# Quantiser without split signs and two tiles in turns in the last feed-forward part; key products in quarters, ahead of their shift, in the local attention

## The reference

```python
_GRID = [0.0, 0.5, 1.0, 1.5, 2.0, 3.0, 4.0, 6.0]
def fp4_quant_dequant(x):          # blocks of 16 along the last dimension
    scale = max(abs(xb)) / 6.0, at least 1e-12
    xn = xb / scale
    q = _GRID[searchsorted(_MID, abs(xn))] * sign(xn) * scale
gate = fp4_linear(x, w_gate)       # 128 -> 352
y = fp4_linear(x, w_up)            # 128 -> 352
h = silu(gate) * y
return fp4_linear(h, w_down)       # 352 -> 128
```

```python
bk, bv = look_around(bk), look_around(bv)     # the window before and the own one
sim = einsum('bhwid,bhwjd->bhwij', bq, bk)
mask = (i < j) | (i > j + WINDOW) | (j == -1)
attn = softmax(where(mask, -max, sim))
out = einsum('bhwij,bhwjd->bhwid', attn, bv)
```

## Time and profile before

| | us |
|---|---|
| median of 3 runs | 4181.39 |
| lowest and highest | 4177.72, 4183.64 |
| the profiled execution's own time | 4167.43 |
| its span (first to last instruction) | 4165.7 |
| TensorE busy (72% of the span) | 3015.8 |
| VectorE busy (61%) | 2557.0 |
| ScalarE busy (35%) | 1448.0 |
| GpSimd busy (19%) | 787.8 |

### The profile page before, as it was taken

The page is one execution under the profiler, slowest core; times in us unless marked ns, Lnnn a source line. Parts: engine busy times, 40 slices in busy tenths (PEclk is TensorE's granted clock), DMA queues, the critical chain, the costliest instruction groups (busy, mean ns, idle before and its releaser), DMA issues. The chain is left out here.

```text
span 4165.7 us, 87048 instructions
## 1 busy us (share of the span) xinstructions
PE 3015.8 (72%) x34526; PEld 2091.1 (50%) x34526; DVE 2557.0 (61%) x7026; ACT 1448.0 (35%) x2873; POOL 787.8 (19%) x759
## 2 busy tenths in 40 slices
PE   4567887886547788788554778878856477787885
PEld 3434565654434456565443445656535244565653
DVE  6674565557676456555757745764575764566457
ACT  4134433422404344342240434434224044343421
POOL 3132211101213221110121322121012132111110
PEclk7579999997657899899765889999976588999996
DMA  1011000000001100000000110000000011000000
GB/s 37 6 38 30 14 3 2 14 20 1 7 6 38 30 14 3 2 14 20 1 7 6 40 30 12 3 2 18 16 1 7 6 40 30 11 3 2 19 14 6
DMA packets 65264, 59.65 MB, mean 14 GB/s; under 512 B 16403, under 2 KB 54212, under 8 KB 64838
## 3 DMA queue, kind: packets, MB, share of 16 engines
q1 hardware_dynamic: 63606, 53.24, 4.7%
q10 hardware_dynamic: 1232, 0.61, 0.1%
HBM read 36.29 MB, written 2.10 MB: 9 GB/s over the span
## 5 line engine op out<-in xcount | busy, mean ns | idle before, releaser
L157 POOL TENSOR_TENSOR ln_rstd<-ln_var_eps,neghalf 128x4 f32<-128x4 f32 x128 | 130.1, 1017 | 1223.6 <-DVE ln_var_eps L169 1188.5
L1188 POOL TENSOR_TENSOR l1t_ss<-l1t_ss,neghalf 128x16 f32<-128x16 f32 x64 | 243.7, 3808 | 478.8 <-DVE l1t_ss L1222 478.8
L2103 ACT ACTIVATE l2r_P<-l2r_bank_score 128x512 f32<-128x512 f32 x320 | 173.7, 594 | 176.3 <-PE l2r_bank_score L1825 176.3
L2103 ACT ACTIVATE l2a_P<-l2a_bank_score 128x512 f32<-128x512 f32 x320 | 173.7, 594 | 168.7 <-PE l2a_bank_score L1825 168.7
L1395 PE MATMUL l1t_ring<-l1f_qkv,x_normT 128*128 128x512 f32 x384 | 218.8, 699 | 13.1 <-ACT x_normT L1095 13.1
L1995 DVE CUSTOM_DVE_ANT_0 l2r_masked<-l2r_bank_ring,l2r_neg_wide 128x512 bf16<-128x512 f32 (+1 forms) x256 | 148.7, 622 | 76.7 <-PE l2r_bank_ring L1794 76.4
L1995 DVE CUSTOM_DVE_ANT_0 l2a_masked<-l2a_bank_ring,l2a_neg_wide 128x512 bf16<-128x512 f32 (+1 forms) x256 | 149.0, 622 | 73.9 <-PE l2a_bank_ring L1794 72.6
L1825 PE MATMUL l2a_bank_score<-l2a_q_head,l2a_k_head 32*128 32x128 f32 x2560 | 188.3, 284 | 2.4 <-DMA l2a_q_head<-l2a_shiftT 1.0
L1794 PE MATMUL l2r_bank_ring<-l2r_k_head,l2r_q_head 32*128 32x128 f32 x2432 | 174.6, 286 | 19.9 <-DVE l2r_m L1995 9.8
L1794 PE MATMUL l2a_bank_ring<-l2a_k_head,l2a_q_head 32*128 32x128 f32 x2432 | 176.7, 286 | 16.4 <-DVE l2a_m L1995 7.1
L1825 PE MATMUL l2r_bank_score<-l2r_q_head,l2r_k_head 32*128 32x128 f32 x2560 | 186.0, 282 | 2.6 <-DMA l2r_q_head<-l2r_shiftT 1.2
(11 more groups left out here) (616 smaller groups left out, 7949.6 us busy)
## 6 DMA issues: line engine op xcount, KB each, us to landing
l1t_v_low<-l1t_v SPq DMA_DIRECT2D x112, 130.0 KB, 2.3
l2e_w<-in_L_ffn_w SPq DMA_DIRECT2D x96, 128.0 KB, 2.3
l1f_qkv<-in_L_ffn_wqkv SPq DMA_DIRECT2D x8, 768.0 KB, 4.5
l1f_tables<-in_l_tables SPq DMA_DIRECT2D x8, 512.0 KB, 6.0
l1f_w<-in_L_ffn_w SPq DMA_DIRECT2D x8, 341.0 KB
x_in<-in_L_attn_hidden_states SPq DMA_DIRECT2D x10, 256.0 KB, 3.5
l1f_wo<-in_L_ffn_wo SPq DMA_DIRECT2D x8, 256.0 KB, 4.8
l2a_q_head<-l2a_shiftT SPq DMA_DIRECT2D x128, 2.0 KB
```

The source lines that it names most:

```text
L157: pool.tensor_tensor(b.rs[:, p, :], b.ve[:, p, :], b.neghalf[:, 0:NT], ALU.pow).then_inc(s["post_rstd"] if post else s["pre_rstd"], 1)
L1188: pool.tensor_tensor(ss[:, n % 2], ss[:, n % 2], b.neghalf[:, 0:2 * H8], ALU.pow).then_inc(s["rn_ready"], 1)
L2103: act.activation(self.P[:, use % self.P_RING].rearrange("k h q -> k (h q)"), self.score_bank(h, g)[:, :], ACT.Exp, scale=self.scale).then_ ...
```

## The change

In the last feed-forward part the quantiser is replaced by `fp4_in_turns`, which takes one or two tiles and gives every step to each tile in turn; a step waits for the last step of its own tile only (`Turns`). It rounds the signed value, without the magnitude and without putting the sign back. The tiles go in the groups (0), (1, 2), (3, 4), (5, 6), (7). The gate and up product of tile 0 stand ahead of the second sequence's transposes, and TensorE and ScalarE follow the groups. The up products now wait for h itself (`h_ready`) and not for the quantised h.

In the local attention the keys of a score tile change places: its rows 0 to 63 are the first 64 keys of the own tile, which all 128 queries use, its rows 64 to 127 the last 64 keys of the tile before for the first 64 queries, and the second 64 keys of the own tile for the others. So a chunk takes, for each row half of the array, one product of 64 keys with 128 queries and two with 64. Mask and key products come first and are placed before the output of the tile before; the shift is added last, in `subtract`. The masks `neg_k` and the layout of `v_low` follow.

```diff
+def fp4_in_turns(dve, turns, jobs, ready, dst_read=()):
...
+    for i, (src, dst, am, inv, v, pw, r) in jobs:
+        turns.wait(i)
+        turns(i, dve.tensor_scalar(pw.bitcast(U32), v.bitcast(U32), EXPONENT, None, ALU.bitwise_and))
+    for i, (src, dst, am, inv, v, pw, r) in jobs:
+        turns.wait(i)
+        turns(i, dve.tensor_scalar(pw, pw, 1.0, magic, ALU.max, ALU.mult))
+    for i, (src, dst, am, inv, v, pw, r) in jobs:
+        turns.wait(i)
+        turns(i, dve.scalar_tensor_tensor(r, v, 1.0 - 2.0 ** -24, pw, ALU.mult, ALU.add))
...
@@ l1_ffn_attention, sync
-                sync.dma_start(v_low[64:128, p, j], v[0:64, p, j]).then_inc(s["v_low_ready"], 16)
+                sync.dma_start(v_low[0:64, p, j], v[0:64, p, j]).then_inc(s["v_low_ready"], 16)
...
@@ l1_ffn_attention, tensor
             def scores(n):
                 j, p = tiles[n]
-                pe.wait_ge(s["q_ready"], n + 1)
-                pe.wait_ge(s["k_ready"], n + 1)
-                pe.wait_ge(s["shiftT_ready"], n + 1)
                 if n:
                     pe.wait_ge(s["p_ready"], 2 * n)
...
+                pe.wait_ge(s["q_ready"], n + 1)
+                pe.wait_ge(s["k_ready"], n + 1)
+                for c in range(CHUNKS):
+                    at = 128 * c
+                    for half, here, keys, queries in ((0, 0, j * 128 + 64, slice(0, 128)), (1, 0, j * 128, slice(0, 64)),
+                                                      (1, 64, j * 128 + 128, slice(64, 128))):
+                        for u in range(2):
+                            rows = slice(64 * u, 64 * u + 64)
+                            pe.matmul(s_bank[u][64 * half:64 * half + 64, at + here:at + queries.stop],
+                                      k[rows, p, c, keys:keys + 64], q[rows, n % 2, c, queries], start=False, stop=True,
+                                      skip_group_check=True)
+
+            def subtract(n):
+                p = tiles[n][1]
+                pe.wait_ge(s["shiftT_ready"], n + 1)
...
             for n in range(T):
-                scores(n)
+                subtract(n)
...
+                if n + 1 < T:
+                    scores(n + 1)
                 if n:
                     turn_output(n - 1)
...
@@ l3_ffn, scalar
+            gate(0)
+            for k, members in enumerate(groups):
+                for n in groups[k + 1] if k + 1 < len(groups) else ():
+                    gate(n)
+                for n in members:
+                    copy_h(n)
...
@@ l3_ffn, tensor
+            turn_x(0)
+            gate_up(0)
+            turn_x(1)
+            for k, members in enumerate(groups):
+                for n in groups[k + 1] if k + 1 < len(groups) else ():
+                    gate_up(n)
+                for n in members:
+                    turn_h(n)
+                for n in members:
+                    down(n)
```

More of the change, by code:

```diff
@@ L814, with __init__, wait, __call__ @@
 FP4 = Quantizer(16, 6.0, 1e-12, 1.0 / 2, signed=False)
+class Turns:
+    def __init__(self, eng, sem, n):
+        self.eng, self.steps, self.done = eng, Steps(eng, sem), [0] * n
+    def wait(self, i):
+        if self.done[i]:
+            self.eng.wait_ge(self.steps.sem, self.done[i])
+    def __call__(self, i, ins):
+        self.steps(ins)
+        self.done[i] = self.steps.n
+def fp4_in_turns(dve, turns, jobs, ready, dst_read=()):
+    block, unit = 16, 1.0 / 2
+    magic = 1.5 * 2.0 ** 23 * unit
+    def blocks(a):
+        return a.rearrange("p (n k) -> p n k", k=block)
+    def spread(a):
+        return a.unsqueeze(2).to_broadcast([a.shape[0], a.shape[1], block])
+    jobs = list(enumerate(jobs))
+    for i, (src, dst, am, inv, v, pw, r) in jobs:
+        turns.wait(i)
+        turns(i, dve.tensor_reduce(am, blocks(src), AX, ALU.max, apply_absolute_value=True))
+    for i, (src, dst, am, inv, v, pw, r) in jobs:
+        turns.wait(i)
+        turns(i, dve.tensor_scalar(am, am, 1.0 / 6.0, 1e-12, ALU.mult, ALU.max))
+    for i, (src, dst, am, inv, v, pw, r) in jobs:
+        turns.wait(i)
+        turns(i, dve.reciprocal(inv, am))
+    for i, (src, dst, am, inv, v, pw, r) in jobs:
+        turns.wait(i)
+        turns(i, dve.tensor_tensor(blocks(v), blocks(src), spread(inv), ALU.mult))
+    for i, (src, dst, am, inv, v, pw, r) in jobs:
+        turns.wait(i)
+        turns(i, dve.tensor_scalar(pw.bitcast(U32), v.bitcast(U32), EXPONENT, None, ALU.bitwise_and))
+    for i, (src, dst, am, inv, v, pw, r) in jobs:
+        turns.wait(i)
+        turns(i, dve.tensor_scalar(pw, pw, 1.0, magic, ALU.max, ALU.mult))
+    for i, (src, dst, am, inv, v, pw, r) in jobs:
+        turns.wait(i)
+        turns(i, dve.scalar_tensor_tensor(r, v, 1.0 - 2.0 ** -24, pw, ALU.mult, ALU.add))
+    for i, (src, dst, am, inv, v, pw, r) in jobs:
+        turns.wait(i)
+        turns(i, dve.tensor_tensor(r, r, pw, ALU.subtract))
+    for i, (src, dst, am, inv, v, pw, r) in jobs:
+        turns.wait(i)
+        if dst_read and dst_read[i][1]:
+            dve.wait_ge(*dst_read[i])
+        dve.tensor_tensor(blocks(dst), blocks(r), spread(am), ALU.mult).then_inc(ready, 1)
 def l0_ffn_weights(nc, ctx, b, a):
@@ L1031, in l1_ffn_constants @@
         own(pool.tensor_copy(m[64:128, :], w.neg_low[64:128, :]))
+    own.settle()
+    own(pool.memset(w.neg_low[:], 0.0))
+    keep(w.neg_low[:, 0:64], [[-1, 64]], -64, 1, fill=MASKED)
     for first, m in enumerate(w.neg_k):
-        keep(m[:], [[0, 2], [-1, 64]], 0, 1, fill=MASKED)
-        keep(m[:], [[0, 2], [1, 64]], 64, -1, fill=MASKED)
-        if first:
-            keep(m[:, 0:64], [[0, 64]], -64, 1, fill=MASKED)
+        keep(m[:, 64:128], [[-1, 64]], 0, 1, fill=MASKED)
+        keep(m[:, 64:128], [[1, 64]], 64, -1, fill=MASKED)
+        keep(m[:, 0:64], [[1, 64]], 0, -1, fill=MASKED)
+        if not first:
+            own.settle()
+            own(pool.tensor_copy(m[64:128, 0:64], w.neg_low[64:128, 0:64]))
     keep(w.sel[:], [[-1, H8], [0, 128]], 0, 1, ALU.not_equal, 1.0)
@@ L1184, in _ @@
             own(pool.memset(k_bf[:, :, :, 0:64], 0.0))
-            own(pool.memset(v_low[0:64, :, 0], 0.0))
+            own.settle()
+            own(pool.memset(v_low[64:128, :, 0], 0.0))
+            own.settle()
             for n in range(T):
@@ L2911, in copy_h, with gate, turn_x @@
                                ACT.Copy).then_inc(s["hT_ready"], 1)
-            for n, (j, p) in enumerate(tiles):
+            def gate(n):
+                p = tiles[n][1]
                 act.wait_ge(s["gate_ready"], n + 1)
+                if n >= PAIR:
+                    act.wait_ge(s["h_ready"], n + 1 - PAIR)
                 act.activation(silu[:, p, :], g_ps[p][:, 0:I_FFN], ACT.Silu).then_inc(s["silu_ready"], 1)
-                if n >= 1:
-                    copy_h(n - 1)
-            copy_h(len(tiles) - 1)
+            gate(0)
[4 more added lines that the diff above has]
+                    copy_h(n)
         @block.tensor
         def _(pe):
-            transpose_x(pe, b, s["xq_ready"], s["xT_psum"], xq, t_ps)
-            pe.wait_ge(s["xT_ready"], PAIR)
+            def turn_x(p):
+                pe.wait_ge(s["xq_ready"], p + 1)
+                for j in range(NT):
+                    last = pe.transpose(t_ps[p][:, j * 128:(j + 1) * 128], xq[:, p, j, :], b.ident[:])
+                last.then_inc(s["xT_psum"], 1)
             def gate_up(n):
                 j, p = tiles[n]
-                if n >= PAIR:
+                if j == 0:
+                    pe.wait_ge(s["xT_ready"], p + 1)
+                else:
                     pe.wait_ge(s["silu_ready"], n + 1 - PAIR)
@@ L2945, in _, with down @@
                 last.then_inc(s["hT_psum"], 1)
+            def down(n):
+                j, p = tiles[n]
                 pe.wait_ge(s["hT_ready"], n + 1)
```

72 lines of the change are left out of this document (37 added, 35 removed).

## The result

| | before | after |
|---|---|---|
| median of 4 runs, us | 4182.52 | 4004.16 |
| lowest and highest | 4177.72, 4191.53 | 3997.83, 4005.72 |
| the profiled execution's own time | 4167.43 | 4003.84 |

The ratio of the times is 0.9568, with a 95% interval of 0.9549 to 0.9588: 4.3% faster. The direction was forecast; 4004 lies 49 us under the forecast of 4053 and outside the range (4030 to 4092). The profiled executions differ by 163.6 us, where the forecast had 128.

The account below looks back on a forecast made before the run. VectorE was taken to bound the last feed-forward part and TensorE the local attention. 60 us (four passes) plus 68 us (eight stages) made 128 us: 4039 us profiled, 4053 us median, range 4030 to 4092.

Parts of the forecast that it names:

- 1.5 us a stage for the place: Attention, mask and keys earlier: about 0.8 us in tile 0, half in tile 1, 0.3 in the last, nothing mid-stage.
- the quarters: Attention, key products on 64 x 64 quarters: 1.06 us instead of 1.93, 0.87 less a tile, 7.0 in 8 tiles.
- The x quantiser: Last part: without the two sign steps on x, 1.06 us less for each of two sequences, 2.1 us a pass.
- the first product: Last part: tile 0's products ahead of the second sequence let VectorE start 1.06 us earlier.
- The pair: Last part, two tiles in turns: 17 waits of 0.115 us saved, 0.05 given back, 7.1 us a pair.
- The 0.6 us for TensorE's half clock: Last part: allowance of 0.6 us lost a pass for gate and up products coming late at half clock.
- The 14.0 us carried over unchanged: Whole kernel: the profiled execution's 14.0 us under the median was taken to stay the same after the change.
- Quarters taking turns: Attention rival: fp32 quarters do not overlap, key products take 1.8 us, kernel 4103 us; chance 0.13.
- quarters without overlap: Attention rival: load and stream of one row half never overlap, 3 us, kernel 4177 us, no change; chance 0.01.
- Turns save nothing: Last part rival: the pipe empties after every step anyway, 5.8 us a pass missing, kernel 4076 us; chance 0.03.
- VectorE's chain: Attention rival, joined with TensorE bounding the last part at half clock: 12 and 17 us lost, 4082 us; chance 0.12.
- The half clock in the attention: Attention rival: TensorE falls to 1.2 GHz, 5 us a tile; with 35 tiles the kernel takes 4228 us; chance 0.02.

Follow-up runs that it names:

- The place alone: Kernel before with mask and key products early and the shift last, keys still on 64 x 128 halves with the old masks: 4116.1 us, ratio 0.9877.
- the transposes first: Kernel after with the output's transposes ahead of mask and key products: 3960.5 us; a second run also puts silu ahead of the second sequence's copy: 3949.2 us.
- its repeat: The kernel after run once more, unchanged, as measure for the runs made with it: 4002.7 us, ratio 0.9608 to the kernel before.
- the quarters in place: Kernel before with key products in quarters and the new masks, all score products still behind the shift's transpose: 4099.6 us, ratio 0.9843.
- the bank's wait first: Kernel before with one wait moved: ahead of the mask TensorE waits for the free score bank first and the shift last: 4143.5 us, ratio 0.994.

## Why the prediction was wrong

In the main its mechanisms held; but one term that was put at nothing was not nothing, and the sizes below were wrong, all to one side. 128 us were forecast between the profiled executions and 163.6 came (35.6 more), and the offset to the median adds 13.7: 49 us.

- **"In the middle of a stage TensorE only changes the order", and 1.5 us a stage for the place: the step that failed, the largest error.** The place alone gave 4.2 us a stage. The waits of tile 0 and tile 1 were given up in full (1.13 and 1.14 us between the same instructions) where I had 0.8 and 0.4; I had looked up tile 0's wait and guessed tile 1's, although its row (0.97 us idle) stood in the same trace. In the middle, which was put at nothing, 0.20 us a tile went, 0.11 of it shown to be the order of the waits. The 0.88 us that the prediction read there was an uncommon tile's, 0.78 the usual one's. The last two tiles gained 0.29 us each beyond the quarters; I had counted one. Together with the quarters, which were right (0.84 against 0.87 a tile, 7.1 against 7.0 a stage), a stage gave 10.2 to 10.9 us and not 8.5; with the clock's share the 8 stages gave 87.8 and not 68.
- **The last part, 60 us, gave 68.5.** The x quantiser (2.1) and the first product (1.06) were right to 0.05 us. The pair was 6.86 us, not 7.1. The one wait that I kept is there (the step behind the second h starts 0.55 us after it, the second h 0.43 us after the first), but the other 17 saved 0.128 us each and not 0.115 (9.04 - 6.86 = 2.18), and the short steps, for which I gave 0.05 us back, saved as much as the long ones: L849 for both tiles takes 0.20 us, where a single one takes 0.21. The 0.6 us for TensorE's half clock was not needed (the 8.5 us of the difference are 2.9 from this pair, 2.4 from the allowance, 2.3 from stalls of TensorE which the kernel before already had, 38.18 or 37.76 us from first to last h instead of 37.4, and which pairs remove as well, and 0.9 behind the last h). The allowance also rested on a misreading: 4.37 and 2.58 us of work are those of stretches of 5 us, and a tile was 5.34 us, so two tiles are some 9.3 us at half clock and 5.5 at full, not 8.7 and 5.2.
- **"The 14.0 us carried over unchanged": wrong.** It was one set's spread: the kernel after has 0.3 us between its profiled execution and its median. The medians of the unchanged kernel moved by 14 us between sets. The sets of the experiments ran on three different chips, so nothing here tells a chip's share from chance.
- **The untouched parts gave 7.3 us**, net: the part whose clock is shown above gave 9.5 in the four passes, the others differ both ways by less; my 12 us of spread for the clock covered this, but not all of it and the offset at once. About 21 of the 49 us are this and the offset, which the edit doesn't explain, and 28 are the two stages.
- **The rivals.** Quarters taking turns (1.8 us) and quarters without overlap (3 us) are excluded by 1.09 us. "Turns save nothing" (9.04 us a pair) is excluded by 6.86, and with it, for steps of this size, the rule of the Trainium skill that was weighed (VectorE: DVE Perf Modes, "The DRAIN you can't avoid"): the trace does not agree. The section itself also says that an operation which is not held starts earlier, and the steps without a wait do so here (0.44 us against 0.56). VectorE's chain did come level with TensorE's in the attention, as the row of its reciprocal shows, but cost nothing; with 0.8 us less of waiting in front of it, in the run with the transposes first, it still kept up at 9.94 us a tile. The half clock in the attention took single tiles (12.6 us at a mean of 0.86), no stretches.
- **Why the range failed.** Its low end added tile 0's wait alone. I had bounded the losses one by one, but no gain of the place, nor what removed stalls of before were worth, so no case stood under 4030.

## What to carry to other kernels

When independent work is put ahead of a hand-over in an order written by hand, list every wait for that hand-over in the trace, the first two tiles' and the last's too, and count each in full where that engine is the bound: here such waits were worth 4.2 us a stage for one move and 4.7 for the next. Put the wait that ends last behind the others, and give every step of a dependent chain to two tiles in turn. Before a median is forecast from a profiled execution, compare several sets of runs of the unchanged kernel, for their spread can be as large as an edit.

## What the runs showed of the hardware that was not expected

- Products in fp32 on four 64 x 64 quarters ran side by side: 48 records in 1.09 us, where 32 records on two 64 x 128 halves took 1.93 us. A quarter has 8 records of 128 moving columns or 16 of 64, so that is 0.14 or 0.07 us each.
- A wait already met costs TensorE 0.11 us more if it stands behind the one that holds it than if it stands ahead (0.78 against 0.67 us from the shift's transpose to the mask).
- Most of the quantiser's VectorE steps on 352 columns start 0.44 us after the last when they take turns and 0.56 when they wait for it (L858 and L861 0.25 and 0.38); L849 with 22 columns 0.10 and 0.21. Over all steps the saving is 0.11 to 0.15 us, and it does not grow with the size.
- In the two traces of the kernel after and its repeat 11 of the 64 middle tiles took 12.6 us instead of 10.92, at a mean clock of 0.86. In the two with the transposes first no middle tile was long, but in 5 of their 16 stages the last tile took 9.0 us instead of 7.5, at 0.81. The runs with the quarters in place and with the bank's wait first had no long middle tile either. Nothing here shows what decides it.
